# Attention with a two-pass softmax: VectorE adds the causal mask while it takes the row maxima of the wider diagonal tiles

## The reference

```python
x = x + layernorm(attn(layernorm(x), wq, wk_down, wv_down, wk_up, wv_up, wo))
x = x + layernorm(moe(layernorm(x), ...))    # 32 experts, 6 of them per token, 16 anchors, 1 shared
# inside attn, per head:
scores = (q . k) * scale
scores = where(causal, scores, finfo.min)    # key position <= query position
probs = softmax(scores)
y = probs @ v
```

## Time and profile before

| what | value |
|---|---|
| runs, median (all) | 446.71 us (446.71, 447.78, 442.34) |
| profiled execution, its own time | 443.81 us |
| its span, first to last instruction | 442.0 us |
| mean granted TensorE clock | 0.961 |
| busy share of the span | PE 92%, PE weight loads 60%, DVE 73%, POOL 58%, ACT 52% |
| attention, first pass to last block | about 16 to 236 us |
| expert stage | about 236 to 442 us |

### The profile page before, as it was taken

One profiled execution on the slowest core, in us unless ns is written; L12 is line 12 of the kernel. 1 busy time (PEld: TensorE's weight loads), 2 busy tenths in 40 slices (PEclk: granted clock), 3 DMA queues, 4 the chain that ended last, 5 costly groups with the idle time before them and its releaser, 6 DMA issues.

```text
span 442.0 us, 7088 instructions
## 1 busy us (share of the span) xinstructions
PE 406.8 (92%) x2212; PEld 263.4 (60%) x2212; DVE 324.3 (73%) x792; ACT 229.9 (52%) x444; POOL 254.4 (58%) x266
## 2 busy tenths in 40 slices
PE   7969899998899899999999999998999999999981
PEld 6656455644354453444546777776766777778860
DVE  6866897869975686452838985769996899576661
ACT  3435353664254466565475546675556555565641
POOL 6118667564935457465376655577554766277642
PEclk9888999999589999999999999999999999899996
DMA  6087171333050022050000000000000000000000
GB/s 202 4 196 105 18 180 37 123 56 53 3 71 2 3 41 33 1 73 4 2 1 2 0 1 1 0 6 20 1 1 1 25 0 0 2 1 24 1 0 24
DMA packets 9891, 14.57 MB, mean 33 GB/s; under 512 B 1216, under 2 KB 5504, under 8 KB 9472
## 3 DMA queue, kind: packets, MB, share of 16 engines
q1 hardware_dynamic: 9568, 13.49, 15.3%
q10 hardware_dynamic: 288, 0.64, 0.5%
HBM read 6.26 MB, written 1.05 MB: 17 GB/s over the span
## 4 chain that ended last, share of the span: by engine, by line
PE 64%; DVE 19%; DMA 5%; issue 4%; POOL 3%; ACT 3%; SPq 1%; POOLq 0%; ACTq 0%; DVEq 0%
PE ps L1226 9%; PE ps L1248 8%; PE ps L1136 7%; PE acc L1262 7%; PE ps L1137 6%; PE ps L1138 6%; PE total L1272 4%; PE acc L1333 4%; DVE ps L1086 4%; DMA qst<-q_lo 3%; PE acc L1335 3%; PE acc L1334 3%; DVE h_lo L1091 3%; DVE cw L1075 2%; PE ps L1229 2%
## 5 line engine op out<-in xcount | busy, mean ns | idle before, releaser
L733 POOL TENSOR_TENSOR silu<-silu,cwb 128x512 f32<-128x512 f32 x80 | 103.5, 1298 | 70.5 <-ACT silu L860 69.9
L971 DVE TENSOR_REDUCE nmax_h<-ps 128x1 f32<-128x512 f32 (+3 forms) x152 | 92.3, 654 | 42.9 <-PE ps L1229 33.7
L832 ACT ACTIVATE probs<-ps 128x512 f32<-128x512 f32 (+1 forms) x152 | 80.1, 579 | 62.8 <-PE ps L1250 34.5
L698 POOL TENSOR_TENSOR probs<-probs 128x768 f32<-128x768 f32 (+2 forms) x48 | 78.3, 1645 | 49.5 <-PE acc L1262 33.6
L1226 PE MATMUL ps<-kst,qst 96*128 96x512 f32 (+3 forms) x192 | 67.8, 414 | 6.5 <-DMA qst<-q_lo 5.4
L1091 DVE TENSOR_TENSOR h_lo<-ps,h_hi 128x512 fp32r<-128x512 f32 (+1 forms) x84 | 57.0, 684 | 19.1 <-ACT h_hi L870 18.7
L1086 DVE TENSOR_TENSOR ps<-silu,ps 128x512 f32<-128x512 f32 (+1 forms) x84 | 57.5, 689 | 15.3 <-POOL silu L733 11.3
L870 ACT ACTIVATE h_hi<-ps 128x512 fp32r<-128x512 f32 (+1 forms) x84 | 50.0, 598 | 35.5 <-DVE ps L1086 34.1
L1136 PE MATMUL ps<-xT_hi,w_hi 128*128 128x512 f32 x164 | 66.5, 406 | 0.9 <-ACT silu L860 0.9
L860 ACT ACTIVATE silu<-ps 128x512 f32<-128x512 f32 x80 | 47.6, 598 | 34.6 <-PE ps L1138 27.9
L1137 PE MATMUL ps<-xT_lo,w_hi 128*128 128x512 f32 x164 | 64.8, 395 | 0.0
(11 more groups left out here) (175 smaller groups left out, 555.3 us busy)
## 6 DMA issues: line engine op xcount, KB each, us to landing
qst<-q_hi SPq DMA_DIRECT2D x14, 256.0 KB, 5.2
qst<-q_lo SPq DMA_DIRECT2D x7, 256.0 KB, 6.9
x_sb<-in_attn_x SPq DMA_DIRECT2D x4, 256.0 KB, 6.5
raw<-in_ffn_w_gate SPq DMA_DIRECT2D x1, 1024.0 KB, 8.9
raw<-in_ffn_w_up SPq DMA_DIRECT2D x1, 1024.0 KB, 4.8
raw<-in_ffn_w_down SPq DMA_DIRECT2D x1, 1024.0 KB, 5.0
result<-x_sb SPq DMA_DIRECT2D x4, 256.0 KB, 2.3
kst<-k_hi SPq DMA_DIRECT2D x6, 128.0 KB, 3.2
```

Of the source, the lines that this page charges most:

```text
L698: nc.gpsimd.tensor_tensor(into, into, probs[:, k % KTBUF, js, cols], ALU.add).then_inc(added, 1)
L733: nc.gpsimd.tensor_tensor(silu[:, k % HRING, :], silu[:, k % HRING, :], cwb[:, m % 2, t // ET, :], ALU.mult).then_inc(scaled_ready, 1)
L832: nc.scalar.activation(probs[:, k % KTBUF, j:j + w, CH - cols:CH], bank(full)[:, 0:w * cols].rearrange("p (w c) -> p w c", w=w), ACT.Exp). ...
L971: nc.vector.tensor_reduce(nmax_h[:, n % 2, i, j:j + w, h], bank(full)[:, 0:w * keys].rearrange("p (w k) -> p w k", w=w), AX.X, ALU.max, ne ...
```

## The change

In the first pass, for diagonal tiles that hold one head per bank (i = 2 and 3; 8 per block, 64 in all), the mask matmul L1229 goes. VectorE adds the mask in the instruction that takes the maximum, `tensor_tensor_reduce`: it reads the scores and a bf16 row of zeros that ends in the 128 mask columns, multiplies the sum by -1, takes the minimum, and writes the negated sums back over the scores in PSUM. Tiles i = 0 and 1 keep their mask product and the old reduction. GpSimd prepares `mask_row`, 512 columns wide, in place of `mask1` with 128. In the planner these `p1` steps are 16 units (0.16 us) cheaper, the maxima cost what they did, and `consts` costs 290 units instead of 220.

```diff
+def masked_by_max(ev):
+
+    _, n, i, _, h, wide = ev
+    return h == BLOCKS[n][1] and wide == 1
...
-    step("POOL", ("consts",), 220, 0)
+    step("POOL", ("consts",), 290, 0)
...
-            step("PE", ev, wide * max(19, cols * 23 // CH) + 16 * (h == c), rank, *qs, *ks, ("consts",), bank=1, until=peak)
-            step("DVE", peak, 15 + wide * cols * 104 // 1000, rank, ev, n >= 2 and ("nm_split", n - 2))
+            step("PE", ev, wide * max(19, cols * 23 // CH) + 16 * (h == c and wide > 1), rank, *qs, *ks, ("consts",), bank=1, until=peak)
+            step("DVE", peak, 15 + wide * cols * 104 // 1000, rank, ev, n >= 2 and ("nm_split", n - 2), ("consts",))
...
-        mask1 = sb("mask1", [P, P], BF16)
+        mask_row = sb("mask_row", [P, CH], BF16)
...
-                    link(nc.gpsimd.memset(mask1[:], 0.0))
-                    nc.gpsimd.affine_select(out=mask1[:], in_=mask1[:], compare_op=ALU.is_ge, fill=MASK, base=0,
+                    link(nc.gpsimd.memset(mask_row[:], 0.0))
+                    nc.gpsimd.affine_select(out=mask_row[:, CH - P:], in_=mask_row[:, CH - P:], compare_op=ALU.is_ge, fill=MASK, base=0,
...
                     dve.wait_ge(scores_full, SCORES[full])
+                    if masked_by_max(full):
+                        dve.wait_ge(masks, 2)
+                        scores = bank(full)[:, 0:keys]
+                        nc.vector.tensor_tensor_reduce(scores, scores, mask_row[:, CH - keys:CH], -1.0, BIG, ALU.add, ALU.min,
+                                                       nmax_h[:, n % 2, i, j:j + 1, h]).then_inc(max_ready, 1)
+                        continue
...
-                                                start=(r == 0), stop=(h < c))
-                    if h == c:
-                        last = nc.tensor.matmul(s[:, :, P * i:P * i + P], ident_bf[:], mask1[:].unsqueeze(1).to_broadcast([P, w, P]), start=False, stop=True)
+                                                start=(r == 0), stop=(h < c or masked_by_max(ev)))
+                    if h == c and not masked_by_max(ev):
+                        last = nc.tensor.matmul(s[:, :, P * i:P * i + P], ident_bf[:], mask_row[:, CH - P:].unsqueeze(1).to_broadcast([P, w, P]), start=False, stop=True)
```

## The result

The changed kernel takes 447.2 us (median of four runs, 446.6 to 447.9); the kernel before, run on the same chip, took 444.5 (441.0 to 447.8). The ratio of the two is **1.0089, 95% interval 1.0045 to 1.0132**: some 4 us slower, where I had forecast 2.7 us faster. 447.2 lies inside the range, but the sign was wrong.

A forecast was written before the change was run, and what follows sets the result against it. TensorE was taken to set the pace in most places, VectorE in some. Terms -4.8 + 1.7 + 1.0 - 0.6 summed to -2.7 us, giving a forecast of 442.5 us, range 435 to 451 us.

The forecast's parts named there:

- The order around the end of the routing: Block 3's shift comes later behind block 2's `recip` and `yl`: +1.0 us, bounds -1.5 and +4.
- Start of the expert stage: Chunk 1's logits ahead of block 7's second pass let about half its route steps run earlier: -0.6 us, bounds 0 and -1.3.
- Block 3's late shift: Block 3's shift, at 117.78 before, starts 1.3 us later; part of a term taken as +1.0 us.
- Rival 3: Block 3's late shift idles TensorE, with more half clock; the order costs 4 us: 444 to 448 us, chance 0.18.
- The masks: 64 mask products leave TensorE at 0.12 us each, counted in blocks 2 to 7: -4.8 us, bounds 0 and -7.7.
- The fused instruction: Mask, add and minimum on VectorE for 64 tiles costs 0.10 us more a tile, mostly in idle time: +1.7 us.
- Rivals 2 and 4: New VectorE instruction at half rate, 448 to 452 us, chance 0.12; or write-out delayed, 442.5 to 445.5 us, chance 0.10.
- rival 4: VectorE's write-out starts only when the main instruction has left the pipe, 0.18 us a tile: 442.5 to 445.5 us, chance 0.10.
- Rival 1: TensorE paces all of blocks 2 to 7 and the order helps: -7.7 us, 436 to 439 us, chance 0.20.
- the last tile of blocks 4 to 7: VectorE's last fused tile ahead of the split in each of four blocks lies on the path: 0.4 us.
- block 2's queries: Near block 1's end, TensorE's wait for these queries grows beyond 1.61 us, so block 1's saved masks are worth nothing.

The follow-up runs named there:

- old instructions: Mask products and plain maxima of the kernel before, in the changed kernel's order: 446.0 us, 1.0074; with chunk 1's routing behind block 7's output scaling 442.0 us, 0.9951.
- routing last: Changed kernel, its planner holding chunk 1's routing until block 7's output scaling is planned: 440.4 us, 0.9899 of the kernel before.
- short adds: GpSimd's adds at the ends of blocks 3's and 4's second pass in pieces of 128x192: kernel before 441.5 us, 0.9942; exchange in its order 438.0 us, 0.9887.
- VectorE's half: Kernel before with fused add and maximum on 64 tiles, mask products kept: 455.0 us, 1.0253; with GpSimd's adds cut into 192-column pieces 442.2 us, 0.9965.
- old order: Changed instructions in the order of the kernel before on every engine, the planner given its old costs: 448.6 us, 1.0105 of the kernel before.

## Why the prediction was wrong

- **What failed is the step "The order around the end of the routing" together with "Start of the expert stage".** I looked for the order's price at block 3 and called the earlier logits a gain of 0.6 us. They are the loss. I had +1.0 - 0.6 = +0.4 us for the two. With the routing taken out from in front of block 7's reciprocal the changed kernel measures 0.9899 in place of 1.0089, 1.9% or 8.4 us less, some 4 us below the kernel before where I had forecast 2.7: the rest of the sum did not make it slow. In its trace VectorE's queue holds the reciprocal 5.5 us behind the routing, slowed by GpSimd, and half clock follows. With the old instructions the same line is worth 1.2% (1.0074 against 0.9951), there without a trace that shows the wait. I had named neither what is queued behind the routing nor GpSimd's adds beside it; in the kernel before showed a quiet place.
- **Block 3's late shift**: forecast 1.3 us later and +1.0 at the end. It came 5.8 us later, behind a transpose of the routing weights before which TensorE stood 6.60 us (the weights were there at 119.0; the wait ended with block 3's last maximum, 121.3 to 122.0, which stood behind `recip` and `yl` of block 2), and it was made good: the reciprocal of block 3 starts at 154.58 against 153.62, shift 4 at 146.62 against 147.09. Rival 3 gave the right time for the wrong reason: with routing last the shift is as late and the kernel 1% faster than before.
- **The masks**: 0.12 us a product was right where starts are read, -4.8 us at the end was not. With short adds their removal alone gave 0.9934 against 0.9942, 0.4 us less, give or take 2.8. Windows full to 27 of 28 us made me take TensorE's work for the path almost whole. In the traces of these two runs, from shift 1 to shift 7, TensorE's idle time rises from 6.3 to 8.3 us and the stretch is 2.6 us shorter; with one trace of each, more can't be said.
- **The fused instruction**: 0.10 us a tile forecast, 0.05 from start to start measured; some 30 ns on the main one (712 against 682, 576 against 548) and 139 for the second, which overlaps. On the path +1.7 us forecast, 1.0 measured (0.9965 against 0.9942, an interval of some 3 us each way). Rivals 2 and 4 fall on the 0.65. The page that rival 4 names goes on to say that an op that is not held starts earlier (the Trainium skill, "VectorE: DVE Perf Modes", section "The DRAIN you can't avoid"); the trace agrees, since the fused instructions start 0.08 us before the one ahead has ended (0.73 long, 0.65 apart). Rival 1's 436 to 439 us came in neither order as it stood, and only with short adds (438.0).
- **The exchange as a whole**: -4.8 + 1.7 = -3.1 us forecast. Measured with each order's defect out of the way: 0.9887 against 0.9942 and 0.9899 against 0.9951, twice half a per cent or 2.3 us. Each pair alone has an interval of about 3 us to either side, and so have the halves, which one by one give nothing (-0.4 and +1.0 us). Whether that is more than noise, no run shows; in the traces from shift 1 to shift 7 the kernel before with short adds takes 172.3 us, without masks 169.7, with VectorE's half 174.8 and with both 168.9, the last with 3.4 us less of half clock.
- **The split** appears in my sum only as "the last tile of blocks 4 to 7". The earlier trace rows showed TensorE waiting there for the split, and I did not ask why an instruction on 16 columns made it wait. In the old order, that alone turns -1.1% into +1.0%. In the changed kernel the new order had moved the split of blocks 4 and 5 off the adds (0.17 us each), so this loss was not in the 447.2 us; the routing was. That is a gain of the new order that I had not priced: with routing last it gives the old instructions 0.9951, what short adds give them in the old order (0.9942). Only block 7's split was caught there (1.81 us, TensorE waited 1.50).
- **The head**: TensorE fell to half clock from 19 us to 33 in place of 29 to 36, which the forecast did not have, and block 2's queries were waited for 2.49 us in place of 1.61, as forecast. What either costs at the end, no run tells from noise.

What stays open: the half clock in the changed kernel from 57 to 64 us, which no run took away by itself; whether the routing would still hold the reciprocal up with GpSimd's adds beside it cut short; and what the exchange is worth to better than 3 us.

## What to carry to other kernels

An instruction on a few columns that sits directly ahead of a hand-over (a split, a cast, a rank) is to be checked in the trace for durations far above its own: if it is 0.17 us in one block and 1.7 in another, its place beside another engine's long instruction can be worth more than the work that one moves about. When costs in a planner change, look for what the new order puts in front of the instruction that ends a stage, in the same queue, before pricing the exchange itself. And a wait of 3 us on TensorE should be priced with the half clock behind it; filling it with useless products shows how much that is.

## What the runs showed of the hardware

- VectorE's small split instructions on operands in SBUF, the cast and the subtraction with two inputs, lasted until GpSimd's running add ended: 0.17 us became 1.72 beside adds of 1.8 us and 0.51 beside adds of 192 columns (0.59 us). The fused instruction, with one operand in PSUM, was never caught (539 to 733 ns over all 64 in the changed kernel), though 28 of them began with 0.3 us or more of a GpSimd instruction still to run.
- Which of two instructions 0.1 us apart came first decided 1.7 us of wait.
- In a wait of 2.7 us at shift 5 (to 180.5 us) the granted clock fell to 0.50, from 179 to 190 us; the same wait with 2.3 us of useless products in it kept 1.00. In the kernel before, waits of 1.34 and 0.95 us at these shifts kept 1.00 too.
